# Expert outputs weighted on their way out of PSUM and added to the residual rows in DRAM by accumulating scatters, in place of a combining last phase

## The reference

```python
probs = jax.nn.softmax(logits, axis=-1)
top_w, top_i = jax.lax.top_k(probs, TOP_K)              # TOP_K = 2
top_w = top_w / jnp.sum(top_w, axis=-1, keepdims=True)
...
for e in range(NUM_EXPERTS):                            # 12 experts, F = 320
    h = jax.nn.silu(x @ w1[e].T) * (x @ w3[e].T)
    out = out + h @ w2[e].T * cw[:, e:e + 1]            # cw: the weight of expert e for each token
...
x = _layernorm(x + out, axis=-1)
```

## Time and profile before

| | |
|---|---|
| median of 3 runs | 755.45 us (755.4 to 756.53) |
| the profiled execution | 753.75 us, its span in the trace 751.9 us |
| attention, until the last store to x2_d is issued | 0 to 446.2 us |
| sorting, until the first matmul of tile 0 | 446.2 to 464.7 us |
| 43 tiles, until the copy of the last one | 464.7 to 719.0 us |
| last phase | 719.0 to 751.9 us |
| busy in 464.7 to 717.0 | PE 247.4, DVE 111.7, ACT 61.1, POOL 95.4 us of 252.3 |

### The profile page before, as it was taken

One profiled execution on the slowest core, in us unless ns is written; L12 is line 12 of the kernel. 1 busy time (PEld: TensorE's weight loads), 2 busy tenths in 40 slices (PEclk: granted clock), 3 DMA queues, 4 the chain that ended last, 5 costly groups with the idle time before them and its releaser, 6 DMA issues. The chain is left out here.

```text
span 751.9 us, 17839 instructions
## 1 busy us (share of the span) xinstructions
PE 715.3 (95%) x6227; PEld 519.3 (69%) x6228; DVE 500.0 (67%) x1102; ACT 342.1 (45%) x695; POOL 304.7 (41%) x336
## 2 busy tenths in 40 slices
PE   9999899999999999999899988999999999999994
PEld 4777677777878778687765777666666666666641
DVE  3857968879788697796878887444444444444477
ACT  3865654756556566586465212222222222222264
POOL 0574465464654645645412002243433444334210
PEclk9999999999999999999999999999999999999997
DMA  8824465354652545536310026455465555522865
GB/s 326 311 70 150 132 215 180 92 170 134 200 182 87 179 142 169 183 133 219 112 72 15 30 94 224 175 196 208 146 218 217 214 210 199 206 84 84 335 239 194
DMA packets 40124, 126.78 MB, mean 169 GB/s; under 512 B 4224, under 2 KB 4608, under 8 KB 38144
## 3 DMA queue, kind: packets, MB, share of 16 engines
q1 hardware_dynamic: 31024, 99.49, 38.1%
q0 software_dynamic: 6880, 22.55, 8.9%
q10 hardware_dynamic: 2160, 3.93, 1.5%
HBM read 81.13 MB, written 44.83 MB: 168 GB/s over the span
## 5 line engine op out<-in xcount | busy, mean ns | idle before, releaser
L1088 DVE COPY_PREDICATED ST<-msk,pS 128x256 f32<-128x256 uint8 x224 | 121.2, 570 | 51.4 <-issue 24.7
L763 POOL TENSOR_TENSOR piece_parts<-piece,piece_parts 128x1024 f16<-128x1024 f32 x48 | 103.7, 2161 | 96.2 <-ACT piece_parts L708 96.2
L1581 PE MATMUL pH<-ring,xgh 128*128 x344 | 103.0, 300 | 3.9 <-issue 2.0
L757 POOL TENSOR_TENSOR RL<-RL,AM 128x256 f32<-128x256 f32 x96 | 72.1, 751 | 78.1 <-ACT RL L700 72.3
L1582 PE MATMUL pH<-ring,xgh 128*128 x344 | 102.9, 299 | 0.0
L1583 PE MATMUL pH<-ring,xgl 128*128 x344 | 102.9, 299 | 0.0
L1893 POOL DMA_INDIRECT y_scratch<-ysb,sidx x43 | 42.8, 996 | 128.7 <-DVE ysb L1809 125.8
L401 PE MATMUL pS<-RL 64*128 64x64 f32 (+2 forms) x1536 | 89.1, 265 | 0.0
L1793 DVE TENSOR_TENSOR hid<-pH,sil 128x320 f32<-128x320 f32 x43 | 21.2, 492 | 98.0 <-ACT sil L1663 49.1
L401 PEld LDWEIGHTS pS<-RL 64*128 64x128 f32 (+1 forms) x1536 | 84.4, 178 | 2.2
L741 DVE TENSOR_TENSOR RL<-RL,AM 128x256 f32<-128x256 f32 x96 | 70.2, 731 | 9.7 <-ACT RL L687 7.8
(11 more groups left out here) (254 smaller groups left out, 1536.6 us busy)
## 6 DMA issues: line engine op xcount, KB each, us to landing
piece<-in_w_experts SPq DMA_DIRECT2D x48, 512.0 KB, 5.0
w_split_scratch<-piece_parts SPq DMA_DIRECT2D x48, 512.0 KB, 3.9
ring<-w_split_scratch SPq DMA_DIRECT2D x12, 2048.0 KB
yin<-y_scratch SPq DMA_DIRECT2D x16, 512.0 KB, 12.7
out_x<-X SPq DMA_DIRECT2D x8, 512.0 KB, 2.8
x_scratch<-X ACTq DMA_DIRECT2D x15, 256.0 KB, 2.0
X<-in_x SPq DMA_DIRECT2D x2, 1536.0 KB, 18.1
RL<-in_wxT SPq DMA_DIRECT2D x4, 256.0 KB, 5.2
```

The lines of the kernel that those rows point to most:

```text
L757: g.tensor_tensor(next_kept(k, lv, 0), kept(key, k, lv, 0), by, ALU.mult).then_inc(k_dec, 1)
L763: g.tensor_tensor(piece_parts[buf][:, 1, :], piece[buf][:, :], piece_parts[buf][:, 0, :], ALU.subtract).then_inc(piece_lo, 1)
L1088: v.copy_predicated(out[:, :, :, 0 if lv == 0 else 1, :], msk[:, lv, :, :].rearrange(shape, m=m), pS[:, :, lv * S:(lv + 1) * S].rearrange( ...
L1581: pe.matmul(p[:, 0, 0:F], xgh[par][:, k, :], wh, start=(k == 0), stop=False)
```

## The change

The scatter becomes an adding one. `sum_d` is a second copy of the rows in DRAM, with 128 spare rows for padding places. Each tile's output is multiplied by the token's weight when VectorE takes it out of PSUM, and the scatter adds the rows to `sum_d`. Two scatters may meet the same row, so each waits for the one before. Since VectorE needs one weight for each place of the tile, `wtop` is stored to DRAM as a table of 4,096 single floats (`w_d`), and a third indirect DMA per tile (`weigh`) gathers 128 of them, two tiles ahead. The last phase loads the sums into `X` and only measures and normalises.

```diff
             def send_x2(t):
                 a.wait_ge(norm2, t + 1)
                 a.dma_start(x2_d[t * P:(t + 1) * P, :], X[:, t, :]).then_inc(x2_out, 16)
+                a.dma_start(sum_d[t * P:(t + 1) * P, :], X[:, t, :]).then_inc(sum_in, 16)
...
         def _(sp):
             sp.dma_start(x2_d[last * P:, :], X[:, last, :]).then_inc(last_out, 16)
+            sp.dma_start(sum_d[last * P:T, :], X[:, last, :]).then_inc(last_sum, 16)
+            sp.dma_start(sum_d[T:, :], X[:, 0, :]).then_inc(last_sum, 16)
...
             for slot in range(1, RING):
                 load(slot, slot)
+            sp.wait_ge(wtop_ready, 1)
+            sp.dma_start(w_d.rearrange("(n p j) o -> p n (j o)", p=P, j=2), wtop[:, :, :]).then_inc(w_stored, 16)
...
-            yv = y_d[0:2 * T, :].rearrange("(n p j) c -> n p j c", p=P, j=2)
...
             for i in range(NT):
-                sp.dma_start(yin[i % YIN][:, :, :], yv[i]).then_inc(y_in[i % YIN], 16)
+                sp.dma_start(X[:, i, :], sum_d[i * P:(i + 1) * P, :]).then_inc(y_in[i], 16)
...
             def copy_out(i, j, par):
                 v.wait_ge(o_full, i + 2)
                 v.wait_ge(y_free[par], j + 1)
-                v.tensor_copy(ysb[par][:, :], pO[:, 0, :]).then_inc(o_out, 1)
+                v.wait_ge(wg_in[par], j * 16 + 16)
+                v.tensor_scalar(ysb[par][:, :], pO[:, 0, :], wgate[par][:, 0:1], None, ALU.mult).then_inc(o_out, 1)
...
+            def weigh(i, par, steps):
+
+                g.tensor_copy(widx[par][:, :], wseli[:, bass.ds(i, 1)]).then_inc(g_step, 1)
+                g.wait_ge(g_step, steps)
+                g.sem_inc(g_waited, 1)
+                g.indirect_dma_start(out=wgate[par][:, :], out_offset=None, in_=w_d,
+                                     in_offset=bass.IndirectOffsetOnAxis(ap=widx[par][:, :], axis=0)).then_inc(wg_in[par], 16)
...
                 g.wait_ge(o_out, i + 2)
+                if not isinstance(i, int) or i:
+                    g.wait_ge(y_sent[1 - par], (sent + par) * 16)
                 g.sem_inc(g_waited, 1)
-                g.indirect_dma_start(out=y_d, out_offset=bass.IndirectOffsetOnAxis(ap=sidx[par][:, :], axis=0),
-                                     in_=ysb[par][:, :], in_offset=None).then_inc(y_sent[par], 16)
+                g.indirect_dma_start(out=sum_d, out_offset=bass.IndirectOffsetOnAxis(ap=sidx[par][:, :], axis=0),
+                                     in_=ysb[par][:, :], in_offset=None, compute_op=ALU.add).then_inc(y_sent[par], 16)
...
+            g.wait_ge(dest_ready, 1)
+            g.wait_ge(w_stored, 16)
+            g.sem_inc(g_waited, 1)
+            for k in range(2):
+                weigh(k, k, counted())
...
             for k in range(AHEAD):
-                fetch(k + AHEAD, k, 2 * k + 1)
-                if k == 0:
-                    g.wait_ge(dest_ready, 1)
-                send(k, k, 2 * k + 2, k // 2)
+                fetch(k + AHEAD, k, counted())
+                send(k, k, counted(), k // 2)
+                weigh(k + 2, k % 2, counted())
```

More of the change, by code:

```diff
@@ L132, in __init__ @@
         self.ones_h = take(P, F16)
-        self.diag = [early[:, i * 2 * P:(i + 1) * 2 * P].rearrange("p (c t) -> p c t", c=2) for i in range(NT - 3)]
 def attention(nc, X, idt, kc, gw, x, wxT, ww, wk, wv, wr, wo, by_feature, ident, masks, consts, gate_w, w_experts, w_split, logitT, early, pA,
-              x2_d, x2_out):
+              x2_d, x2_out, sum_d, sum_in):
     with ExitStack() as ctx:
@@ L1335, in kc_col, with experts @@
     return kc[:, K_AT[k]:K_AT[k + 1]]
-def experts(nc, X, idt, kc, gw, w_split, early, pA, x2_d, x2_out, y_d, out):
+def experts(nc, X, idt, kc, gw, w_split, early, pA, x2_d, x2_out, sum_d, sum_in, w_d, out):
     I32 = mybir.dt.int32
@@ L1395, in experts @@
         ysb = [sb(f"ysb{i}", [P, C]) for i in range(2)]
-        yin = [sb(f"yin{i}", [P, 2, C]) for i in range(YIN)]
+        widx = [sb(f"widx{i}", [P, 1], I32) for i in range(2)]
+        wgate = [sb(f"wgate{i}", [P, 1]) for i in range(2)]
         stats = sb("stats3", [P, NT, 6])
@@ L1427, in experts @@
         last_out = sem("last_out")
+        last_sum = sem("last_sum")
+        w_stored = sem("w_stored")
+        wg_in = [sem(f"wg_in{i}") for i in range(2)]
         w_in = [sem(f"w2_in{i}") for i in range(RING)]
@@ L1445, in experts @@
         y_sent = [sem(f"y_sent{i}") for i in range(2)]
[L1446 to L1449, removed]
+        y_in = [sem(f"y_in{i}") for i in range(NT)]
         terms3 = sem("terms3")
@@ L1625, in _ @@
             down(SLOTS - 1, place(SLOTS - 1))
[L1626 to L1632, removed]
         @block.scalar
@@ L1679, in _ @@
                 tile(i, i % 2, more=i + 2 < SLOTS)
[L1681 to L1686, removed]
             for q, (lo, hi) in enumerate(LAST_GROUPS):
@@ L1836, in terms @@
                 v.scalar_tensor_tensor(nmr[:, at], mv[:, at, 0], -1.0, rstd[:, at], ALU.mult, ALU.mult).then_inc(terms3, 1)
[L1838 to L1844, removed]
-                    u = ON_PE.index(i)
-                    v.wait_ge(y_mixed, u + 1)
-                    v.tensor_tensor(X[:, i, :], X[:, i, :], pMix[u % MIX][:, 0, :], ALU.add).then_inc(y_added, 1)
             def measure(i):
-                v.wait_ge(y_added, i + 1)
+                v.wait_ge(y_in[i], 16)
                 return v.bn_stats(stats[:, i, :], X[:, i, :])
@@ L1912, in _ @@
                 for k in range(AHEAD):
-                    fetch(j * AHEAD + (k + AHEAD), k, j * (2 * AHEAD) + (2 * k + 1))
-                    send(j * AHEAD + k, k, j * (2 * AHEAD) + (2 * k + 2), j * (AHEAD // 2) + k // 2)
-            steps = 2 * AHEAD * rounds
+                    at = j * (3 * AHEAD) + (2 + 3 * k)
+                    fetch(j * AHEAD + (k + AHEAD), k, at + 1)
+                    send(j * AHEAD + k, k, at + 2, j * (AHEAD // 2) + k // 2)
+                    weigh(j * AHEAD + (k + 2), k % 2, at + 3)
+            steps = 2 + 3 * AHEAD * rounds
             for i in range(rounds * AHEAD, SLOTS):
                 if i + AHEAD < SLOTS:
-                    steps += 1
-                    fetch(i + AHEAD, i % AHEAD, steps)
-                steps += 1
-                send(i, i % AHEAD, steps, i // 2)
+                    fetch(i + AHEAD, i % AHEAD, counted())
+                send(i, i % AHEAD, counted(), i // 2)
+                if i + 2 < SLOTS:
+                    weigh(i + 2, i % 2, counted())
 def program(nc, x, wxT, ww, wk, wv, wr, wo, by_feature, gate_w, w_experts, ident, masks, consts, out):
@@ L1933, in program @@
           nc.psum_tensor("pA", [P, 2, 512], F32) as pA,
-          nc.semaphore("x2_out") as x2_out):
+          nc.semaphore("x2_out") as x2_out, nc.semaphore("sum_in") as sum_in):
         attention(nc, X, idt, kc, gw, x, wxT, ww, wk, wv, wr, wo, by_feature, ident, masks, consts, gate_w, w_experts, w_split, logitT, early, pA,
-                  x2_d, x2_out)
-        experts(nc, X, idt, kc, gw, w_split, early, pA, x2_d, x2_out, y_d, out)
+                  x2_d, x2_out, sum_d, sum_in)
+        experts(nc, X, idt, kc, gw, w_split, early, pA, x2_d, x2_out, sum_d, sum_in, w_d, out)
 def constants():
@@ L1962, in constants @@
     packed = [np.broadcast_to(a, (P, n)) for a, n in zip(
[L1963 removed]
+        [e, np.arange(SLOTS), np.arange(P), step, token, p + (T + 1), p < np.arange(P), lower, p % GATE_W == e],
         K_WIDTHS)]
```

34 lines of the change are left out of this document (20 added, 14 removed).

## The result

On one chip the changed kernel took 816.89 us at the median of four runs (813.42 to 821.58), the kernel before 755.99 (four runs, 755.4 to 758.47): a ratio of 1.082, interval 1.079 to 1.086. Forecast were 761 us and a range of 749 to 788. The sign came true, the size did not: +61 us where +5 were forecast.

The account below looks back on a forecast made before the run. TensorE was taken to bound the tiles, VectorE the last phase. Terms -11.9 + 4.7 - 2.3 + 8.4 + 6.3 = +5.2 us, added to the median of 755.45, gave 761 us; range 749 to 788.

Parts of the forecast that it names:

- Last phase, -11.9: From last copy out of PSUM to the end: 21.0 us instead of 32.9, ScalarE setting the pace, a gain of 11.9.
- The weight table, +8.4: Ahead of the tiles: table store held behind ring loads, scatter 0 8.4 us late; upper bound 84 ns a piece, 10.8 us.
- Rivals 1 and 5: Weight table: 1, store not held by ring loads, 752 us, chance 0.17; 5, table at its upper bound, 770 us, 0.08.
- The third DMA, +4.7 - 2.3: In the tiles: GpSimd sets the pace at 5.98 against 5.857 us, 4.7 lost; 2.3 not lost through the copy's lead.
- The adding instruction, taken at 1.00 us: GpSimd in each tile: an adding scatter's instruction takes 1.00 us like gather and plain scatter; each tenth more costs 3.8.
- Rival 3: GpSimd in the tiles: the adding instruction takes 1.5 us, describing a destination read too; +19, 780 us, chance 0.17.
- Adding scatters beside ring loads, +6.3: Nine scatters beside ring loads land after 5.9 us, 0.7 over the 5.2 us of room: 6.3 us, range 0 to 13.5.
- Rival 2: Adding scatters in the tiles: extra traffic so short that no scatter waits; 6.3 falls away, 754 us, chance 0.12.
- Rival 4: Scatters in the tiles: every add lands after 6.5 us, making 7.3 a tile; +49 in place of 6.3, 804 us, chance 0.10.
- Stores in the attention, taken as hidden: ScalarE's 15 extra stores covered by its idle time in the attention; without that cover they cost 5.1 us.
- Padding tiles: The five tiles behind scatter 38: TensorE sets the pace again, since GpSimd has no fetch left; no extra time.
- GpSimd does idle in a tile: Sign against the forecast: if GpSimd still idles in a tile, the sequencer overlaps its waits.

Follow-up runs that it names:

- third_dma_ahead_six: Changed kernel with plain scatters into two tensors, no wait for the former scatter, weight gather kept, gathers six tiles ahead: 768.38 us, 1.022 of the kernel before.
- third_dma_alone: Changed kernel with plain scatters into two tensors, no wait for the former scatter, weight gather kept, gathers four ahead: 810.43 us, 1.078 of the kernel before.
- no_reloads: Changed kernel without the nine loads of ring places that fall into the tiles: 795.45 us, 1.056 of the kernel before.
- no_weigh_ahead_six: Changed kernel with weights gathered for the first two tiles only and rows gathered six tiles ahead, wait kept: 793.96 us, 1.057 of the kernel before.

## Why the prediction was wrong

*Last phase, -11.9: right.* Measured -11.6, by the steps named: VectorE measures all groups and normalises only the last two blocks, ScalarE starts 4.65 us behind the copy (forecast 4.5) and sets the pace. Its timeline after:

```profile
797.46 2.93 ACT L1646 ACTIVATE X<-X,nmr,rstd 128x512 f32<-128x512 f32 x4 [0.66 <-DVE nmr L1828]
800.30 0.19 ACT L1642 ACTIVATE rstd<-mv 128x4 f32<-128x4 f32 x1
800.93 2.93 ACT L1646 ACTIVATE X<-X,nmr,rstd 128x512 f32<-128x512 f32 x4 [0.44 <-DVE nmr L1828]
```

*The weight table, +8.4: right*, +9.5 in the trace. Rivals 1 and 5 fall: the store is held by the ring loads (16.0 us to its landing, 7.6 when it stands ahead of them), and its delay isn't the upper bound. Its pieces themselves take little of the DMA engines; this is DMA activity of after from 478 to 484 us in 40 slices, and its queue of hardware transfers:

```profile
DMA  8997889865310000000000000000000900000000
...
q1 hardware_dynamic: 2056, 0.15, 24.4%
```

2,056 packets took 24.4% of 16 x 6 us, so 11 ns a piece on an engine and not the 84 of the upper bound, and from about 480 on hardly anything moves. By the Trainium skill, DMA: Bandwidth & Descriptors (Specifications), pieces under 512 B are read, modified and written; whatever that costs here lies within the 11 ns. GpSimd's first copy comes at 483.24, some 3 us after the traffic; what fills those is not settled (a single full slice at 482.7 us belongs to the queue that carries instructions).

*The third DMA, +4.7 - 2.3: this is the step that failed.* "GpSimd would have no idle time left and would set the pace" was right and its 5.98 us too (most periods of third_dma_ahead_six). What the step priced was GpSimd's own stream, and it asked what a late *copy out* does. It did not ask what the same slack had bought for the *gathers*. Before, a gather starts 7.5 to 8.4 us ahead of its transposes. Once GpSimd sets the pace, its lead is 4.6 to 5.9 where TensorE comes to wait. A gather issued 1.6 us behind a ring load is used 8.4 us after its start, so the first lead covers it, nearly, and the second doesn't. That is (7.06 - 6.09) x 38 = 37 us where the third DMA stands alone. Of these, 25 are TensorE's waits themselves. The other 12 were not taken apart; TensorE's half clock behind a wait (granted clock 0.68 from 525 to 530 us in third_dma_alone) is one candidate. The prediction had gathers in no term, though the earlier trace rows show one between two scatters and TensorE's timeline shows when its rows are used. Whether the 2.3 us of the copy's lead were kept can't be read off, since the padding tiles behind came out 6.0 us longer.

*The adding instruction, taken at 1.00 us: it is 1.62.* Rival 3, with 0.17 of the chances, had this term and nearly its size (1.5; +19 us); its reason, a read of the destination that must be described too, no run tests. Measured alone it costs (6.72 - 6.09) x 38 = 24 us. By the Trainium skill, Perfetto Trace Analysis (DMA Instruction — SWDGE (GPSIMD)), the end of such an instruction is when the last descriptor is written, not when data has moved; the runs agree in that the instruction takes 1.616 us on average both in the change and without ring loads (no_reloads).

*Adding scatters beside ring loads, +6.3: right place, wrong size.* The room of 5.2 us was held against a landing of 5.9; in the trace the scatter after that of 510.00 starts 8.4 us later, and in no_weigh_ahead_six up to 11. In the change, landings and late gathers lie beside the same loads and cover each other: taking the wait away alone gives 7.36 for 7.34, taking it away with gathers early gives 6.72 for 7.10. Both together are what leaving out the nine ring loads gives back: 277.5 - 255.5 = 22.0 us, 2.4 a load instead of 0.7. Rival 2 (the adds hide) was right for a GpSimd with slack and no wait, 5.89 a tile, and wrong for this one. Rival 4 asked that every landing be over the room; only those beside loads were.

*Stores in the attention, taken as hidden: they are not.* The run of the stores alone has 4 us, within the bound of 5.1; the 3.4 of the traces lie within the spread of that point. *Padding tiles, "at TensorE's pace": no.* The periods behind scatter 38 were 9.32 and 8.27 us; the X loads are issued from 766.02 on, beside the same serial scatters; +6.0. No run leaves those loads out, so their part is argued.

*The signs.* GpSimd does idle in a tile, which was named as a sign that the sequencer overlaps its waits. The trace shows another reason: it waits for a scatter's landing (12 times over the whole span, 36.2 us) or for a copy out that a late gather holds back.

Summed: 3.4 + 9.5 + 54.9 + 6.0 - 11.6 = 62.2. Of the 54.9, 29.0 is GpSimd's longer stream, (6.62 - 5.857) x 38; 22.0 is what the ring loads do to it; the last 3.9 stand in no_reloads as well, 1.2 of them where the loop ends. That the sign came true is no merit of the terms for the tiles: it rested on a balance of +5.2, and each of these terms was too small.

## What to carry to other kernels

Idle time of an engine that issues transfers isn't free to fill: it is what lets a prefetch run ahead. So before a queue is filled up, compare each transfer's lead with its longest landing (the one beside a bulk load), not with its median. When two mechanisms act beside the same event, undoing one can show little, and only the pair gives the sum (7.10 and 7.36 apart, 6.72 together, 7.34 with both). Work moved out of a last phase is saved once (11.6 us here); what takes its place in the tiles is paid in each of them.

## What the runs showed of the hardware

- An adding indirect scatter of 128 rows of 2 KB takes GpSimd 1.62 us, a plain one 0.99 to 1.00, a gather of 128 single words 1.00: the last costs as much as one of 128 rows.
- A gather of 128 rows issued 1.6 us behind a 2 MB load is used by a waiting TensorE 8.4 us after its start; with no such load a gather lands 3.3 us after its issue. In 8.5 us from about that start the load's queue and GpSimd's share the engines (DMA view of after, 507.9 to 516.4 us):

```profile
q1 hardware_dynamic: 140, 2.03, 65.1%
q0 software_dynamic: 278, 0.53, 29.1%
```

  So packets of both queues move in the same stretch, and the load takes most of it. By the Trainium skill, DMA: Bandwidth & Descriptors (Queues, rings and completion order), an engine takes its queues in turn, a packet from each; these rows agree in kind, but don't show the turns.
- 2,048 pieces of 8 bytes went to DRAM at 11 ns of one engine's time a piece. From issue to landing their store took 16.0 us behind two 2 MB loads and 7.6 ahead of them; a store of 256 KB by SP took 3.4 (median of two, in the change).
- Seventeen extra stores of 256 KB ahead of the tiles, 15 by ScalarE in the attention and two by SP, cost 4 us. With 30 by ScalarE the last row store lay at 455.0 to 464.7 in five profiled executions, against 446.6 to 454.7 in ten with 15. Why was not followed further.
